# Second attention of a two-block kernel: the row maxima are subtracted by TensorE, and ScalarE copies the context sums

## The chip, the cores and the metric

The kernel runs on one core of one Trainium2 chip. The metric is the device time of one execution in microseconds (us); before the change it is 456.45 us, the median of three runs (454.14 to 458.66). The engines are TensorE (PE, with its weight loads shown apart as PEld), VectorE (DVE), ScalarE (ACT), GpSimd (POOL) and the DMA queue of SyncE (SP). Each engine works through its own list in order, and semaphores tie the lists together.

## The reference

Two transformer-like blocks, each an attention and a mixture of experts, on 2048 tokens of 128 features (8 batches of 256). The change touches the second block's attention alone:

```python
q = (x @ Wq + bq).reshape(b, h, dh, t)      # h = 16 heads, dh = 8
k = (x @ Wk + bk).reshape(b, h, dh, t)
v = (x @ Wv + bv).reshape(b, h, dh, t)
attn = jnp.einsum('bhdt,bhds->bhts', k, v) * temperature
attn = jax.nn.softmax(attn, axis=-1)
out = jnp.einsum('bhdt,bhts->bhds', q, attn)
```

So each of 8 x 16 heads has a score matrix of 256 x 256, a softmax along its rows, and a product with q. The softmax is computed as exp(score - row maximum) over its row sum.

## The kernel before, in words

**Stages.** First attention, first experts, second attention, second experts. All engines' lists are written out by hand; nothing reorders them. The first experts end at about 200 us of the profile, the second attention's exponentials run until about 330 us, and the second experts fill the rest.

**The second attention's loop.** The 128 heads are taken in 32 groups `g` of four heads `j`. A group has two halves of two heads; one half's scores fill two PSUM banks (per head 128 partitions by 2 x 256: `h` is the upper or lower half of the score rows). Three pairs of banks go round (`bank_s1`), so the scores of one half can be written when the exponentials of the half three before it are done. For each half:

- TensorE, `scores` (L1554): four products, two heads by two `h`, contraction over 24 rows, 256 columns each.
- VectorE, `maxima` (L925): one reduction over both banks gives the negated row maxima `nm1` of two heads by two `h`.
- ScalarE (L1208): per head and `h` one exponential of 256 columns with `nm1` as its per-partition bias, and the row sum out of the accumulator, which is a second instruction (ACTIVATION_READ_ACCUMULATOR). So eight such pairs a group.
- VectorE, `denominators` (L933), takes reciprocals of the four heads' sums; GpSimd, `queries` (L526), multiplies them into the weights `qs4`.
- TensorE, `context` (L1566): four products per `h`, each into 32 output partitions of one bank, `BANK_C1`; two calls (`h` = 0 and 1) finish a group.
- VectorE, `outputs` (L940): copies that bank to `O`, from where DMAs take it.

**TensorE's list around the change.** In turn `g` of the loop (L1592): `scores(g+1, 0)`, `context(g-2, 0)`, `scores(g+1, 1)`, `context(g-2, 1)`, and then in some turns one piece of other work (projections, router products, transposes; in the last turn `gate_up(0)` of the second experts comes first). `context(·, 0)` claims `BANK_C1`, that is, it waits until `outputs` of the group before has copied the sums, and then issues four products of ones by ones into the same bank (`dense`, L1301), whose result the context overwrites. VectorE's turn `g` is `outputs(g-3)`, `maxima(g+1, 0)`, `denominators(g-1)`, other work, `maxima(g+1, 1)`. ScalarE's turn is the eight exponentials of group `g`, with other work behind head 1 or head 3 of a few groups (`modulate`, `high_input`, `queries_out`, `weights_out`).

**The start of the loop.** TensorE's list puts `scores(0, 0)`, two steps of the first experts' last products (`down0`), `scores(0, 1)`, three more such steps, `scores(1, 0)` and a projection ahead of turn 0.

Of the kernel before, what the change touches and what calls it, by code (L numbers as in the profile page):

```python
# [17 lines left out]
B, S = 8, 256  # L18
# [15 lines left out]
HPG = 4  # L34
# [12 lines left out]
def two_block_adaln(nc, a, out, scratch):  # L47
# [4 lines left out]
    with ExitStack() as ctx:  # L52
# [31 lines left out]
        ident = sb("ident", [128, 128])  # L84
        ones = sb("ones", [128, 128])
# [17 lines left out]
        def ex1(g, j):  # L103
# [48 lines left out]
        nm1 = sb("nm1", [128, 4, HPG, 2]); Z1 = sb("Z1", [128, 4, HPG, 2])  # L152
# [17 lines left out]
                 "kvs_ready", "s1_ps", "nm1_ready", "e1_ready", "rz_ready", "qs_ready", "c1_ps",  # L170
# [252 lines left out]
        def _(pool):  # L423
# [117 lines left out]

            clear(0)
# [31 lines left out]
        def _(dve):  # L574
# [360 lines left out]
            def outputs(g):  # L935
                b = g // GPB
                dve.wait_ge(s["c1_ps"], g + 1)
                if b >= 2 and g % GPB == 0:
                    dve.wait_ge(ao_out[b - 2], 16 * HPG)
                v.tensor_copy(O[:, b % 2, g % GPB, :], P[:, BANK_C1, 0:S]).then_inc(s["o1_ready"], 1)  # L940

# [3 lines left out]
            for g in range(NG):  # L945
                if g >= 3:
                    outputs(g - 3)
# [35 lines left out]
            outputs(NG - 3)  # L983
# [3 lines left out]
            for n in range(NP * C1):  # L987
                p, i = divmod(n, C1)
                if n in (1, 2):
                    outputs(NG - 3 + n)  # L990
# [33 lines left out]
        def _(act):  # L1024
# [176 lines left out]

            for g in range(NG):
                for j in range(HPG):
                    act.wait_ge(s["nm1_ready"], 2 * g + j // 2 + 1)
                    if g >= 4 and j == 0:
                        act.wait_ge(s["c1_ps"], g - 3)
                    for h in range(2):
                        last = sc.activation(ex1(g, j)[:, h * S:(h + 1) * S],  # L1208
                                             P[:, bank_s1(g, j), h * S:(h + 1) * S],
                                             ACT.Exp, bias=nm1[:, g % 4, j, h:h + 1], accum_out=Z1[:, g % 4, j, h:h + 1])  # L1210
                    last.then_inc(s["e1_ready"], 1)
                    if j == 1 and g == 7:
                        modulate(2, NP - 1)
# [18 lines left out]

            for n in range(NP * C1):
                p, i = divmod(n, C1)
                if i == C1 - 1:
# [30 lines left out]
        def _(pe):  # L1266
# [280 lines left out]
            def scores(g, half):  # L1547
# [3 lines left out]
                for j in (2 * half, 2 * half + 1):  # L1551
                    claim(bank_s1(g, j), "e1_ready", HPG * g + j + 1)
                    for h in range(2):
                        last = mm(P[:, bank_s1(g, j), h * S:(h + 1) * S],  # L1554
                                  KS[32 * j:32 * j + 3 * DH, p % 2, g % GPP, h * D:(h + 1) * D],
                                  VS[32 * j:32 * j + 3 * DH, p % 2, g % GPP, :], start=True, stop=True)
                    last.then_inc(s["s1_ps"], 1)
# [200 lines left out]
```

## Time and profile before

| | |
|---|---|
| median of 3 runs | 456.45 us (454.14 to 458.66) |
| span of the profiled execution, first to last instruction | 453.7 us |
| TensorE busy | 405.5 us (89%) |
| VectorE busy | 360.9 us (80%) |
| ScalarE busy | 329.2 us (73%) |
| GpSimd busy | 253.0 us (56%) |

The page gives the profiled execution's span and no other time of it; the median of the runs is 2.75 us above the span. Busy shares are means over stages with different limits, so the second attention has to be read by itself, from views of 200 to 330 us. In a timeline row the first number is the start in us from the span's start, the second the duration; instructions of one line that follow each other are merged (`x4`). A matmul's recorded end is modelled, and successive matmuls overlap: how fast they follow each other is read from start to start.

### The profile page before, as it was taken

To read this page: it belongs to the slowest core of one execution; us is meant where nothing else is said; L and a number is where in the kernel's file an instruction comes from. 1 tells how busy PE (TensorE), PEld (TensorE's weight loads), DVE (VectorE), ACT (ScalarE), POOL (GpSimd) and SP (SyncE) were. 2 spreads that over 40 slices of the span, in tenths; PEclk is the share of its full clock that TensorE was granted. 3 is DMA by queue.
4 is the path that set the end of the run, shared out by engine and by line. 5 is a ranking of instruction groups with operands and counts; after the bars stand their busy time and mean duration, and the time that the engine had idled before them with its cause. 6 is when DMAs were issued, how large, how long until landed. Compare 5 with 4: busy or idle time off the path is not lost.

```text
span 453.7 us, 7973 instructions
## 1 busy us (share of the span) xinstructions
PE 405.5 (89%) x2328; PEld 272.9 (60%) x2328; DVE 360.9 (80%) x891; ACT 329.2 (73%) x898; POOL 253.0 (56%) x276
## 2 busy tenths in 40 slices
PE   7979878899699798977888888989999999999994
PEld 6667666677487586743333333434467777788782
DVE  5768795876998969869879798898866779778763
ACT  4366558789597686778899899999974575676551
POOL 3302248788786785831353456445357866566653
PEclk9999998999999999989899899999999999999997
DMA  6730031122034043656735245501416433433640
GB/s 180 230 115 4 0 96 46 46 96 70 24 95 111 28 142 115 139 110 96 174 71 105 84 128 91 147 13 25 116 30 183 115 137 100 138 110 99 190 119 23
DMA packets 45819, 44.72 MB, mean 99 GB/s; under 512 B 5700, under 2 KB 33932, under 8 KB 45776
## 3 DMA queue, kind: packets, MB, share of 16 engines
q1 hardware_dynamic: 45776, 44.21, 36.4%
q8 instruction: 19, 0.31, 0.3%
q14 instruction: 24, 0.20, 0.2%
HBM read 37.76 MB, written 6.44 MB: 97 GB/s over the span
## 4 chain that ended last, share of the span: by engine, by line
ACT 25%; PE 15%; DVE 15%; issue 7%; DMA 5%; POOL 3%; SPq 1%; POOLq 0%; DVEq 0%; ACTq 0%
ACT EX L1208 18%; PE P L1279 4%; PE P L1281 4%; PE P L1280 4%; DVE nm L925 3%; DVE P L994 2%; DVE tmp L1002 2%; POOL hidl L482 2%; DVE tmp L887 2%; DMA G<-gate_rows 2%; DMA KS<-kv_parts 2%; ACT hidh L1159 2%; ACT P L1180 1%; PE P L1301 1%; PE P L1554 1%
## 5 line engine op out<-in xcount | busy, mean ns | idle before, releaser
L482 POOL TENSOR_TENSOR hidl<-tmp,hidh 128x512 fp32r<-128x512 f32 x116 | 149.3, 1297 | 68.7 <-ACT hidh L1159 63.4
L1208 ACT ACTIVATE EX<-P,nm 128x256 f32<-128x256 f32 x256 | 117.2, 526 | 6.1 <-DVE nm L925 5.8
L1159 ACT ACTIVATE hidh<-tmp 128x512 fp32r<-128x512 f32 (+1 forms) x116 | 73.0, 630 | 63.4 <-DVE tmp L1002 31.3
L925 DVE TENSOR_REDUCE nm<-P 128x4 f32<-128x1024 f32 x64 | 78.0, 1220 | 16.1 <-PE P L1554 15.6
L1279 PE MATMUL P<-XH,WH 128*128 128x512 f32 x172 | 74.7, 434 | 4.6 <-DVE tmp L887 3.1
L1281 PE MATMUL P<-XL,WH 128*128 128x512 f32 x172 | 68.1, 396 | 0.0
L1280 PE MATMUL P<-XH,WL 128*128 128x512 f32 x172 | 67.8, 394 | 0.0
L1208 ACT ACTIVATION_READ_ACCUMULATOR EX<-P,nm 128x1 f32 x256 | 66.3, 260 | 0.0
L526 POOL TENSOR_TENSOR qs<-qT,rz 128x128 f32<-128x128 f32 x64 | 25.3, 416 | 69.8 <-DVE rz L933 69.8
L887 DVE TENSOR_TENSOR tmp<-P,G 128x512 f32<-128x512 f32 x64 | 43.3, 685 | 19.5 <-issue 9.6
L1279 PE MATMUL P<-hidh,WH 128*128 128x512 f32 (+1 forms) x124 | 50.9, 410 | 3.8 <-POOL hidl L482 3.1
L1281 PE MATMUL P<-hidl,WH 128*128 128x512 f32 (+1 forms) x124 | 49.9, 402 | 0.0
L1280 PE MATMUL P<-hidh,WL 128*128 128x512 f32 (+1 forms) x124 | 49.6, 400 | 0.0
L1301 PE MATMUL P<-ones 128*128 128x512 bf16 x128 | 34.6, 394 | 14.4 <-DVE O L940 13.1
L994 DVE TENSOR_TENSOR P<-wmod,P 128x512 f32<-128x512 f32 (+1 forms) x52 | 36.0, 693 | 13.1 <-ACT wmod L1248 11.3
L1002 DVE TENSOR_TENSOR tmp<-P,G 128x512 f32<-128x512 f32 (+1 forms) x52 | 36.0, 692 | 13.1 <-DMA G<-gate_rows 5.8
L1279 PEld LDWEIGHTS P<-XH,WH 128*128 128x128 f32 x172 | 32.5, 189 | 17.9 <-DVE tmp L887 5.0
L1180 ACT ACTIVATE P<-P,ub 128x512 f32<-128x512 f32 x64 | 41.6, 651 | 0.4 <-PE P L1281 0.4
L1566 PE MATMUL P<-EX,qs 128*32 128x256 f32 x512 | 41.4, 400 | 0.0
L1554 PEld LDWEIGHTS P<-VS,KS 24*128 24x128 f32 x256 | 21.0, 188 | 29.2 <-issue 14.3
L1248 ACT ACTIVATE wmod<-P 128x512 f32<-128x512 f32 x48 | 28.2, 590 | 13.8 <-PE P L1281 13.7
L1554 PE MATMUL P<-VS,KS 24*128 24x256 f32 x256 | 35.0, 336 | 3.1 <-DMA KS<-kv_parts 2.7
(141 smaller groups left out, 696.0 us busy)
## 6 DMA issues: line engine op xcount, KB each, us to landing
G<-gate_rows SPq DMA_DIRECT2D x56, 256.0 KB, 3.2
kv_parts<-kvs SPq DMA_DIRECT2D x16, 256.0 KB, 4.2
VS<-kv_parts SPq DMA_DIRECT2D x48, 64.0 KB
KS<-kv_parts SPq DMA_DIRECT2D x48, 64.0 KB
G<-gate_rows SPq DMA_DIRECT2D x8, 224.0 KB, 2.9
G<-gate_rows SPq DMA_DIRECT2D x8, 192.0 KB, 3.2
G<-gate_rows SPq DMA_DIRECT2D x8, 160.0 KB, 3.4
X<-in_x SPq DMA_DIRECT2D x4, 256.0 KB, 2.9
```

Source lines behind the costliest of these rows:

```text
L482: nc.gpsimd.tensor_tensor(hidl[:, u % 4, :], source, hidh[:, u % 4, :].bitcast(fp32), ALU.subtract).then_inc(s["low_ready"], 1)
L887: v.tensor_tensor(hidf0[:, u % 4, :], P[:, bank_up(u), :], G[:, q % GR, :], ALU.mult).then_inc(s["bc_read"], 1)
L925: v.tensor_reduce(nm1[:, g % 4, 2 * h:2 * h + 2, :], P[:, bank:bank + 2, :].rearrange("p j (h s) -> p (j h) s", h=2), AX.X, ALU.max, negat ...
L994: v.tensor_tensor(P[k, bank_u(n), :], act_out[k, n % 3, :], P[k, bank_u(n), :], ALU.mult).then_inc(s["u_read"], 1)
L1002: v.tensor_tensor(hidf[k, n % 2, :], P[k, bank_u(n), :], G[k, q % GR, :], ALU.mult).then_inc(s["bc_read"], 1)
L1159: sc.activation(hidh[k, u % 4, :], source[k], ACT.Copy).then_inc(s["high_ready"], 1)
L1180: sc.activation(act_out[:, u % 3, :] if i < C0 else P[:, bank_up(u), :], P[:, bank_up(u), :], ACT.Gelu, bias=ub0[:, e, c:c + 1]).then_inc( ...
L1208: last = sc.activation(ex1(g, j)[:, h * S:(h + 1) * S], P[:, bank_s1(g, j), h * S:(h + 1) * S], ACT.Exp, bias=nm1[:, g % 4, j, h:h + 1], a ...
L1279: mm(P[:, bank, :], WH[k, w:w + m], xh, start=start, stop=False)
L1280: mm(P[:, bank, :], WL[k, w:w + m], xh, start=False, stop=False)
L1281: return mm(P[:, bank, :], WH[k, w:w + m], xl, start=False, stop=stop)
L1554: last = mm(P[:, bank_s1(g, j), h * S:(h + 1) * S], KS[32 * j:32 * j + 3 * DH, p % 2, g % GPP, h * D:(h + 1) * D], VS[32 * j:32 * j + 3 * ...
```

## The change

TensorE now subtracts the maxima. A new call `subtract(g, half)` multiplies an identity matrix (`identr`, rounded to fp32r once by GpSimd) with the negated maxima, each repeated over 256 columns, and accumulates the product on top of the scores in PSUM: two products of 512 columns per half. In TensorE's turn `g`, `subtract(g, 1)` stands behind `context(g-2, 0)` and `subtract(g+1, 0)` behind `context(g-2, 1)`; `subtract(0, 0)` stands ahead of the loop behind the last `down0`. ScalarE's exponentials wait for these products (`f1_ps`) and take no bias. The four `dense` products ahead of each context are gone (those of turns 0 and 1 stay). `outputs` moves from VectorE to ScalarE: in group `g` it stands behind head 0. The scores of a half are issued `h` by `h` over its two heads, where before they went head by head.

```diff
-        nm1 = sb("nm1", [128, 4, HPG, 2]); Z1 = sb("Z1", [128, 4, HPG, 2])
+        nm1 = sb("nm1", [128, 4, HPG, 2], fp32r); Z1 = sb("Z1", [128, 4, HPG, 2])
...
+            nc.gpsimd.tensor_copy(identr[:, :], ident[:, :]).then_inc(s["ident_round"], 1)
             clear(0)
...
             for g in range(NG):
-                if g >= 3:
-                    outputs(g - 3)
                 if g + 1 < NG:
                     maxima(g + 1, 0)
...
+            def outputs(g):
+
+                b = g // GPB
+                act.wait_ge(s["c1_ps"], g + 1)
+                if b >= 2 and g % GPB == 0:
+                    act.wait_ge(ao_out[b - 2], 16 * HPG)
+                sc.activation(O[:, b % 2, g % GPB, :], P[:, BANK_C1, 0:S], ACT.Copy).then_inc(s["o1_ready"], 1)
+
             for g in range(NG):
                 for j in range(HPG):
-                    act.wait_ge(s["nm1_ready"], 2 * g + j // 2 + 1)
+                    act.wait_ge(s["f1_ps"], HPG * g + j + 1)
...
-                                             ACT.Exp, bias=nm1[:, g % 4, j, h:h + 1], accum_out=Z1[:, g % 4, j, h:h + 1])
+                                             ACT.Exp, accum_out=Z1[:, g % 4, j, h:h + 1])
                     last.then_inc(s["e1_ready"], 1)
+                    if j == 0 and g >= 3:
+                        outputs(g - 3)
...
+            def subtract(g, half):
+
+                pe.wait_ge(s["nm1_ready"], 2 * g + half + 1)
+                for j in (2 * half, 2 * half + 1):
+                    mm(P[:, bank_s1(g, j), :], identr[:, :],
+                       nm1[:, g % 4, j, :].unsqueeze(2).broadcast_to([128, 2, S]), start=False, stop=True,
+                       skip_group_check=True).then_inc(s["f1_ps"], 1)
 
             def context(g, h):
                 if h == 0:
                     claim(BANK_C1, "o1_ready", g + 1)
-                    for _ in range(HPG if g < NG - 2 else 0):
-                        dense(BANK_C1)
                     pe.wait_ge(s["qs_ready"], g + 1)
...
             for u in range(NP * STEPS0 - 3, NP * STEPS0):
                 down0(u)
+            pe.wait_ge(s["ident_round"], 1)
+            subtract(0, 0)
             scores(1, 0)
...
                     if g >= 2:
                         context(g - 2, half)
+                    if half == 0:
+                        subtract(g, 1)
+                    elif g + 1 < NG:
+                        subtract(g + 1, 0)
```

TensorE's list in the middle of the second attention, before: from the `dense` products of one turn (L1301) through both contexts (L1566) and the scores between and behind them (L1554).

```order
L1301 MATMUL P<-ones 128x512 [waits o1_ready]
L1301 MATMUL P<-ones 128x512 x3
L1566 MATMUL P<-EX,qs 32x256 [waits qs_ready]
L1566 MATMUL P<-EX,qs 32x256 x3
L1554 MATMUL P<-VS,KS 128x256 [waits e1_ready]
L1554 MATMUL P<-VS,KS 128x256
L1554 MATMUL P<-VS,KS 128x256 [waits e1_ready]
L1554 MATMUL P<-VS,KS 128x256
L1566 MATMUL P<-EX,qs 32x256 x4
L1554 MATMUL P<-VS,KS 128x256 [waits e1_ready]
```

The same stretch of TensorE's list now: contexts are L1581, the identity products L1572, the scores L1561.

```order
L1581 MATMUL P<-EX,qs 32x256 [waits qs_ready,o1_ready]
L1581 MATMUL P<-EX,qs 32x256 x3
L1572 MATMUL P<-nm,identr 128x512 [waits nm1_ready]
L1572 MATMUL P<-nm,identr 128x512
L1561 MATMUL P<-VS,KS 128x256 [waits e1_ready]
L1561 MATMUL P<-VS,KS 128x256 x3
L1581 MATMUL P<-EX,qs 32x256 x4
L1572 MATMUL P<-nm,identr 128x512 [waits nm1_ready]
L1572 MATMUL P<-nm,identr 128x512
L1561 MATMUL P<-VS,KS 128x256 [waits e1_ready]
```

The wait for the copied sums (`o1_ready`) has moved from the ones products to the context itself, and each context is followed by two identity products before the next scores.

ScalarE's list in the same place, one group before (head 0 first):

```order
L1208 ACTIVATE EX,Z<-P,nm 128x256 [waits c1_ps,nm1_ready]
L1208 ACTIVATE EX,Z<-P,nm 128x256
L1208 ACTIVATE EX,Z<-P,nm 128x256 [waits nm1_ready]
L1208 ACTIVATE EX,Z<-P,nm 128x256
L1208 ACTIVATE EX,Z<-P,nm 128x256 [waits nm1_ready]
```

and now, with the copy of the sums as L1199:

```order
L1207 ACTIVATE EX,Z<-P 128x256 [waits c1_ps,f1_ps]
L1207 ACTIVATE EX,Z<-P 128x256
L1199 ACTIVATE O<-P 128x256 [waits c1_ps]
L1207 ACTIVATE EX,Z<-P 128x256 [waits f1_ps]
L1207 ACTIVATE EX,Z<-P 128x256
L1207 ACTIVATE EX,Z<-P 128x256 [waits f1_ps]
```

The copy stands behind the two exponentials of head 0, and every head waits for its identity product where it waited for the maxima.

## Rows read from the trace of the kernel before

**Rows 1.** The page's first line.
```profile
span 453.7 us, 7973 instructions
```
**Rows 2.** Windows: length, busy PE PEld DVE ACT POOL, granted clock, DMA share, GB/s.
```profile
200.00:330.00 130.00, 113.04 (x926) 50.04 (x925) 112.18 (x249) 123.84 (x526) 54.81 (x103) 0.97 0.43 94
...
256.00:260.00 4.00, 3.73 (x24) 1.27 (x24) 2.51 (x6) 3.67 (x16) 2.35 (x4) 0.58 0.00 0
```
**Rows 3.** Timeline, ScalarE: first exponential, first of group 3, last of all.
```profile
200.39 0.47 ACT L1208 ACTIVATE EX<-P,nm 128x256 f32<-128x256 f32 x1
...
213.25 0.48 ACT L1208 ACTIVATE EX<-P,nm 128x256 f32<-128x256 f32 x1
...
329.19 0.45 ACT L1208 ACTIVATE EX<-P,nm 128x256 f32<-128x256 f32 x1
```
**Rows 4.** Timeline, all engines: one turn of the loop, from copy to copy.
```profile
272.38 0.41 DVE L940 COPY O<-P 128x256 f32<-128x256 f32 x1
...
272.86 1.04 PE L1301 MATMUL P<-ones 128*128 128x512 bf16 x4 [0.68 <-DVE O L940]
...
272.97 0.47 ACT L1208 ACTIVATE EX<-P,nm 128x256 f32<-128x256 f32 x1
...
273.41 0.47 ACT L1208 ACTIVATE EX<-P,nm 128x256 f32<-128x256 f32 x1
...
273.82 0.64 PE L1566 MATMUL P<-EX,qs 128*32 128x256 f32 x8
...
274.39 0.50 PE L1554 MATMUL P<-VS,KS 24*128 24x256 f32 x4
...
274.82 0.64 PE L1566 MATMUL P<-EX,qs 128*32 128x256 f32 x8
...
274.97 1.23 DVE L925 TENSOR_REDUCE nm<-P 128x4 f32<-128x1024 f32 x1 [0.37 <-PE P L1554]
...
276.11 0.41 DVE L940 COPY O<-P 128x256 f32<-128x256 f32 x1
```
**Rows 5.** View of one line: ScalarE from PSUM with and without a bias (min/median/max ns).
```profile
L1053 ACT ACTIVATE qT<-P,b0q x4: 684/685/687, 16.9 to 49.0; 128x512 f32<-128x512 f32 x4
L1057 ACT ACTIVATE tqT<-P x4: 597/597/602, 18.8 to 50.9; 128x512 f32<-128x512 f32 x4
```
**Rows 6.** Timeline, TensorE: contexts beside 128x128 fp32r products of 512 columns.
```profile
325.30 0.64 PE L1566 MATMUL P<-EX,qs 128*32 128x256 f32 x8
325.87 0.50 PE L1279 MATMUL P<-XH,WH 128*128 128x512 f32 x1
326.20 0.39 PE L1280 MATMUL P<-XH,WL 128*128 128x512 f32 x1
326.43 0.40 PE L1281 MATMUL P<-XL,WH 128*128 128x512 f32 x1
...
330.61 0.40 PE L1281 MATMUL P<-XL,WH 128*128 128x512 f32 x1
330.94 0.42 PE L1566 MATMUL P<-EX,qs 128*32 128x256 f32 x4
```
**Rows 7.** Timeline: a product and the ScalarE instruction that it releases.
```profile
336.15 0.40 PE L1281 MATMUL P<-XL,WH 128*128 128x512 f32 x1
...
336.59 0.60 ACT L1248 ACTIVATE wmod<-P 128x512 f32<-128x512 f32 x1 [0.63 <-PE P L1281]
```
**Rows 8.** Timeline: other work in the loop on ScalarE, then on TensorE.
```profile
281.77 1.03 ACT L1065 ACTIVATE XT<-P,mcol 128x256 f32<-128x256 f32 x2
...
283.37 0.46 ACT L1208 ACTIVATE EX<-P,nm 128x256 f32<-128x256 f32 x1
...
286.58 1.06 PE L1389 MATMUL P<-rw,XT 128*128 128x9 f32 x8
287.57 0.50 PE L1554 MATMUL P<-VS,KS 24*128 24x256 f32 x4
```
**Rows 9.** Timeline, TensorE: the last product of the first experts.
```profile
202.86 0.40 PE L1281 MATMUL P<-hidl,WH 128*128 128x512 f32 x1
```

More of the change, by code:

```diff
@@ L84, in two_block_adaln @@
         ident = sb("ident", [128, 128])
+        identr = sb("identr", [128, 128], fp32r)
         ones = sb("ones", [128, 128])
@@ L169, in two_block_adaln @@
                  "q1_ps", "q1_sb", "kv_ps",
-                 "kvs_ready", "s1_ps", "nm1_ready", "e1_ready", "rz_ready", "qs_ready", "c1_ps",
+                 "kvs_ready", "ident_round", "s1_ps", "nm1_ready", "f1_ps", "e1_ready", "rz_ready", "qs_ready", "c1_ps",
                  "o1_ready", "gated", "x1_ready", "v_step", "pool_const"]
@@ L540, in attention_residual @@
                 nc.gpsimd.tensor_tensor(X[:, ts, :], X[:, ts, :], AO[:, ts, :], ALU.add).then_inc(s["x1_ready"], 1)
+            pool.wait_ge(s["ld_i"], 16 * N_LD["ld_i"])
+            nc.gpsimd.tensor_copy(identr[:, :], ident[:, :]).then_inc(s["ident_round"], 1)
             clear(0)
@@ L933, in denominators @@
                 v.reciprocal(rz1[:, g % 4, :, :], Z1[:, g % 4, :, :]).then_inc(s["rz_ready"], 1)
[L935 to L940, printed above, removed]
             maxima(0, 0)
@@ L982, in _ @@
             denominators(NG - 1)
-            outputs(NG - 3)
             base = NP * STEPS0
@@ L988, in _ @@
                 p, i = divmod(n, C1)
-                if n in (1, 2):
-                    outputs(NG - 3 + n)
                 dve.wait_ge(s["u_ps"], n + 1)
@@ L1231, in high1 @@
                 high_part(base + n, hidf[:, n % 2, :], rows1(n))
+            outputs(NG - 3)
             for n in range(NP * C1):
                 p, i = divmod(n, C1)
+                if n in (1, 2):
+                    outputs(NG - 3 + n)
                 if i == C1 - 1:
@@ L1550, in scores @@
                     pe.wait_ge(kv_in[p], 16 * 6 * HPG)
-                for j in (2 * half, 2 * half + 1):
+                heads = (2 * half, 2 * half + 1)
+                for j in heads:
                     claim(bank_s1(g, j), "e1_ready", HPG * g + j + 1)
-                    for h in range(2):
+                for h in range(2):
+                    for j in heads:
                         last = mm(P[:, bank_s1(g, j), h * S:(h + 1) * S],
                                   KS[32 * j:32 * j + 3 * DH, p % 2, g % GPP, h * D:(h + 1) * D],
-                                  VS[32 * j:32 * j + 3 * DH, p % 2, g % GPP, :], start=True, stop=True)
-                    last.then_inc(s["s1_ps"], 1)
+                                  VS[32 * j:32 * j + 3 * DH, p % 2, g % GPP, :], start=(h == 0), stop=True,
+                                  skip_group_check=True)
+                        if h == 1:
+                            last.then_inc(s["s1_ps"], 1)
+            def subtract(g, half):
[4 more added lines that the diff above has]
+                       skip_group_check=True).then_inc(s["f1_ps"], 1)
             def context(g, h):
```

## The prediction

> **What bounds the kernel now.** I read the page for the span [rows 1], the windows by stretch to find the stage that the change touches, and there the timeline of each engine. Between 200 and 330 us ScalarE is busy 123.8 of 130 us, TensorE 113.0, VectorE 112.2 [rows 2]: ScalarE is nearest to its limit, but two others are close, and a share does not say which wait ends last. The ends of the stage are the first exponential at 200.39 and the last at 329.19 + 0.45 = 329.6 [rows 3]. Group 3 starts at 213.25, so the 29 groups from there take 116.4 us, 4.01 each.
>
> One turn [rows 4] shows what a turn is made of. ScalarE: an exponential and its accumulator read repeat every 273.41 - 272.97 = 0.44, with rounding 0.45 us, so eight need 3.6. But the copy of the sums comes every 276.11 - 272.38 = 3.73 us, and that is a closed chain: copy 0.41, 0.07 to TensorE, ones 0.96 (272.86 to 273.82), context 0.57 (to 274.39), scores to the start of the maxima 0.58 (274.97), maxima 1.23 less 0.09 overlap, next copy. So today two limits lie side by side, ScalarE at 3.6 and this chain at 3.73; the rest up to 4.01 is other work on ScalarE and VectorE and spells of a slower clock.
>
> **The change, part by part.**
>
> *Bias removed (256 exponentials).* ScalarE's 512 columns out of PSUM take 685 ns with a bias operand and 597 without [rows 5]: 0.09 us. An exponential with its read then repeats every 0.45 - 0.09 = 0.36. No row has an exponential without bias; the bounds are a saving of 0 and of 0.09, and I take 0.09 since the two rows of rows 5 differ in nothing else that ScalarE does.
>
> *Copies moved to ScalarE (32).* One row of 256 columns with bias takes 0.47 [rows 4]; less 0.09 it is 0.38. ScalarE's need per group falls to 8 x 0.36 + 0.38 = 3.26. VectorE loses 32 x 0.41 = 13 us of work; I cost that at nothing, since the new chain below holds no VectorE instruction: counted from the first context of a turn, the scores between the contexts start at 1.24, their maxima are done 0.58 + 1.23 later, at 3.05, and their identity products come in the next turn at 3.94 + 0.57 = 4.5. VectorE's other work has these 1.4 us of room.
>
> *Ones removed, identity products added.* Four products of 512 columns go, four come; TensorE's work hardly changes. But the ones stood where TensorE was waiting anyhow, and the identity products stand between the maxima and ScalarE. What counts is the order: `context(g-2, 0)` waits for the copy, the copy stands behind head 0 of group `g`, head 0 waits for `subtract(g, 0)`, and that stands in TensorE's list behind the whole turn before. This is a closed chain again. Its terms:
>
> - context to the identity products behind it: 0.57 (325.30 to 325.87) [rows 6]
> - identity pair to the next scores: 0.34 (325.87 to 326.20) plus 0.33 for changing over (330.61 to 330.94) [rows 6]
> - scores to the second context: 0.43 (274.39 to 274.82) [rows 4]
> - second context to the second identity pair: 0.57
> - first identity product until its end: 0.50 [rows 6]; to ScalarE 0.04 (336.15 + 0.40 to 336.59) [rows 7]
> - head 0: two exponentials with their reads, 2 x 0.36 = 0.72
> - copy 0.38, and to TensorE 0.06 (VectorE's copy took 0.07, 272.79 to 272.86) [rows 4]
>
> Sum: 0.57 + 0.67 + 0.43 + 0.57 + 0.54 + 0.72 + 0.44 = 3.94 us a turn. ScalarE idles in it twice, about 0.5 and 0.25 us, ahead of head 2 and of head 0; TensorE once, about 0.6, ahead of the first context. So the chain at 3.73 gives way to one at 3.94, and ScalarE's saved 0.36 a group becomes idle time.
>
> Here one rule speaks otherwise. After the change-over the first fp32r product of 512 columns ends 0.50 after its start and the second starts 0.34 later, against 0.39 and 0.23 (326.20 to 326.43) within a run [rows 6]: the new weights are not loaded under the change-over. The Trainium skill, page "TensorE: Matmul & The Clock Gate", section "Back-to-back issue gap", gives N/2.4 + 2.5 ns, 216 ns for 512 columns; by it alone the turn would be about 0.24 us shorter. The row is of the same shape in the same place, so I keep the row; the shorter pair is a rival below.
>
> *Other work in the loop.* ScalarE's, behind head 3: twice a modulation with its rounding, 1.60 us (281.77 to 283.37) [rows 8], less the 0.25 idle: 2.7; two single copies of 0.60 to 0.69 [rows 5], less 0.25 each: 0.8. What stands behind head 1 hides in the 0.5. TensorE's: five pieces like the router products, 0.99 (286.58 to 287.57) [rows 8], of which 0.9 is on top and 0.6 hides: 5 x 0.3 = 1.5; `gate_up(0)` in the last turn, six products at 0.23: 1.5 - 0.6 = 0.9. Together 5.9.
>
> *Start and end.* `subtract(0, 0)` stands behind the last `down0`, which starts at 202.86 [rows 9]: + 0.24 + 0.40 + 0.04 gives a first exponential at 203.5, 3.1 late. The first three groups have no context yet and took 4.29 each before; I put them at 3.65 (two maxima of 1.23 and about 1.2 of other VectorE work), which leaves group 3 at 214.4, 1.2 late. At the end the copy of group 29 stands ahead of ScalarE's work for the second experts: 0.4. Behind that TensorE is nearly full, so a later start is a later end.
>
> *Clock.* Between 256 and 260 us the granted clock is 0.58 on the mean [rows 2]: (1 - 0.58) x 4 / 0.5 = 3.4 us at 1.2 instead of 2.4 GHz. TensorE's part of the new chain is 2.7 of 3.94, so a like spell loses about 3.4 x 2.7/3.94 / 2 = 1.2 us. I count one, with bounds of none and three; ones or identity, TensorE streams as many columns a turn as before.
>
> **Sum** from group 3: 29 x 3.94 = 114.3, + 5.9 + 1.2 = 121.4, against 116.4: +5.0; start and end +1.6: +6.6 us. To be set against: some of the other work falls together on both engines in one turn, where it is paid once; I take 0.7 off. That is +5.9 on a span of 453.7; the page shows nothing of what lies around the span, so I add it to the median of the runs, which is 2.75 above the span: 456.45 + 5.9 = **462.3 us**.
>
> **The rivals.**
>
> *A. The chain as summed*, with its other work and clock between 459 and 466.5: chance 0.56. Of it about 0.10 lies below 461.
>
> *B. The identity pair runs like a pair within a run* (the weights are the same in every pair, and they may already be under way during the change-over): the end comes at 0.39, the second product 0.23 later, turn 3.94 - 0.22 = 3.72, and 29 x 0.22 = 6.4 us less: 455.9. For it: equal weights; against it: the row after the change-over [rows 6]. The Trainium skill's gap, above, would give the same. Its own range, with more or less of the other work hidden, is 453 to 459. Chance 0.22.
>
> *C. Faster: ScalarE sets the pace.* If TensorE reached each identity pair before ScalarE runs dry, a group would take 3.26, and with 5 us of other work 29 x 3.26 + 5 = 99.5 instead of 116.4; with +1.6 that is 441 us. It decides as soon as the chain above is under 3.26, so it needs 0.68 us of its terms to be wrong. For it: ScalarE is the busiest engine of the stage now. The Trainium skill, page "ScalarE: Activation LUTs", section "What ACT_TABLE_LOAD costs", puts about 93 ns on each [128,1] pointer operand, and the trace agrees with 88 [rows 5]. Chance of anything faster than 451.9: 0.10.
>
> *D. The bias costs nothing in the pipeline*, that is, pairs still repeat every 0.45. Then head 0 takes 0.90, and a half of four pairs (1.80) ends after the second identity pair is ready, at 2.91 instead of 2.79 of the turn: 2.91 + 0.90 + 0.44 = 4.25, 29 x 0.31 = 9 us more, 471. Against it: rows 5. Chance 0.07.
>
> *E. More slow-clock spells*, three or four: 466 to 470. Chance 0.05.
>
> **The numbers.** The time is that of A. A measurement of this kernel can tell about 1% from no change, 451.9 to 461.0. Faster: C, 0.10. Same: B and the lower part of A, 0.22 + 0.10 = 0.32. Slower: the rest of A, D and E, 0.46 + 0.07 + 0.05 = 0.58. The range leaves out C and D and a little of B's and E's far ends: 453.5 to 467.5.
>
> **What would show it.** Right: copies (ACT, O<-P) every 3.9 us with the context starting 0.05 behind each; ScalarE idle twice a group, released by the identity products; the accumulator read 0.26 behind its exponential's start; first exponential near 203.5; VectorE's waits on scores grown. Wrong: a second identity product 0.22 behind the first (B), ScalarE without gaps between 230 and 320 (C), exponentials still 0.45 apart (D), or VectorE's maxima as what releases the identity products, which I hold to have 1.4 us to spare.

## The result, and the profile after

The changed kernel takes 470.02 us (median of four executions, 466.91 to 471.82) beside 455.94 for the kernel before on the same chip: 1.029 times as long, 95% interval 1.022 to 1.036. The forecast was 462.3 in a range of 453.5 to 467.5: the sign was right, the size was not, and the median lies outside the range. Executions of one version can differ by some per cent, with their mean granted clock, and a ratio is given from the fast ones alone.

The profiled execution has a span of 465.1 us against 453.7 [rows 1], 11.4 more:

```profile
span 465.1 us, 8077 instructions
```

The ends of the stage on ScalarE are the first exponential, the first of group 3 and the last one; they answer to [rows 3].

```profile
204.63 0.38 ACT L1207 ACTIVATE EX<-P 128x256 f32<-128x256 f32 x1 [1.66 <-PE P L1572]
...
215.31 0.38 ACT L1207 ACTIVATE EX<-P 128x256 f32<-128x256 f32 x1
...
340.46 0.38 ACT L1207 ACTIVATE EX<-P 128x256 f32<-128x256 f32 x1
...
340.82 0.38 ACT L1207 ACTIVATE EX<-P 128x256 f32<-128x256 f32 x1
...
341.17 0.39 ACT L1207 ACTIVATE EX<-P 128x256 f32<-128x256 f32 x1
```

The last exponential ends at 341.6, before at 329.6: 11.9 later, so the whole difference arises up to there, and what follows takes as long as before within 0.5 us. Group 3 begins 2.1 later, and the 29 groups from there take 126.3 us instead of 116.4. The last three rows show the pair of exponential and accumulator read at 0.36 and 0.35 apart; before it was 0.44 [rows 4].

One turn, from one copy of the sums (L1199) to the next; it answers to [rows 4]. L1581 are the contexts, L1572 the identity products, L1561 the scores, L928 the maxima.

```profile
262.89 0.38 ACT L1207 ACTIVATE EX<-P 128x256 f32<-128x256 f32 x1
...
263.62 0.38 ACT L1199 ACTIVATE O<-P 128x256 f32<-128x256 f32 x1
...
264.06 0.64 PE L1581 MATMUL P<-EX,qs 128*32 128x256 f32 x8 [0.56 <-ACT O L1199]
...
264.63 0.70 PE L1572 MATMUL P<-nm,identr 128*128 128x512 f32 x2
...
265.15 0.38 ACT L1207 ACTIVATE EX<-P 128x256 f32<-128x256 f32 x1 [0.42 <-PE P L1572]
265.26 0.50 PE L1561 MATMUL P<-VS,KS 24*128 24x256 f32 x4
...
265.69 0.64 PE L1581 MATMUL P<-EX,qs 128*32 128x256 f32 x8
...
266.26 0.70 PE L1572 MATMUL P<-nm,identr 128*128 128x512 f32 x2
...
266.78 0.39 ACT L1207 ACTIVATE EX<-P 128x256 f32<-128x256 f32 x1
...
267.51 0.38 ACT L1199 ACTIVATE O<-P 128x256 f32<-128x256 f32 x1
```

This is the chain as the forecast has it, term by term: context to identity pair 0.57, pair to scores 0.63 (forecast 0.67), scores to context 0.43, context to the second pair 0.57, to ScalarE 0.52 (0.54), head 0 0.73 (0.72), copy and on to TensorE 0.44. Sum 3.89, and the copies are 3.89 apart. The waits inside the stage answer to it. In these rows stand the engine and line that waited, what ended the wait, us in total, how often, and the longest.

```profile
DVE nm L928 <- PE P L1561: 31.1, 38, 2.9
...
ACT EX L1207 <- PE P L1572: 24.8, 35, 2.6
...
PE P L1581 <- ACT O L1199: 12.8, 17, 2.0
...
PEld P L1572 <- DVE nm L928: 2.3, 5, 0.6
```

ScalarE waits for identity products, TensorE for the copy, and the maxima hardly hold up anybody. What the forecast doesn't have shows in the windows (columns as in rows 2; the granted clock is the number behind POOL's):

```profile
205.00:345.00 140.00, 125.84 (x946) 61.57 (x944) 102.25 (x216) 115.11 (x558) 55.07 (x103) 0.93 0.39 86
247.00:275.00 28.00, 24.68 (x206) 11.56 (x204) 23.85 (x45) 24.34 (x123) 14.14 (x25) 1.00 0.46 112
280.00:290.00 10.00, 8.05 (x62) 4.73 (x54) 5.28 (x10) 8.53 (x39) 3.08 (x7) 0.84 0.44 108
290.00:300.00 10.00, 10.00 (x58) 4.36 (x57) 5.17 (x15) 4.73 (x25) 4.17 (x7) 0.65 0.31 79
300.00:310.00 10.00, 8.99 (x56) 3.81 (x56) 7.70 (x26) 7.65 (x38) 3.81 (x8) 0.69 0.04 13
310.00:320.00 10.00, 8.05 (x55) 3.89 (x48) 6.12 (x15) 6.76 (x30) 2.62 (x7) 0.80 0.02 3
```

From 205 to 280 us TensorE has 2.4 GHz. Between 280 and 320 the mean is 0.745, that is (1 - 0.745) x 40 / 0.5 = 20 us at 1.2 GHz; in the trace these are two spells of 10.2 us, from 286.8 and from 303.9. Between 290 and 300 TensorE has no idle time, and ScalarE is busy less than half of it. The first spell comes 2 us behind this wait of TensorE, which the timeline shows:

```profile
282.14 1.04 ACT L1056 ACTIVATE XT<-P,mcol 128x256 f32<-128x256 f32 x2
...
283.21 0.63 ACT L1066 ACTIVATE XH<-XT 128x512 fp32r<-128x512 f32 x1
...
284.45 0.38 ACT L1199 ACTIVATE O<-P 128x256 f32<-128x256 f32 x1
...
284.89 0.64 PE L1581 MATMUL P<-EX,qs 128*32 128x256 f32 x8 [1.95 <-ACT O L1199]
```

ScalarE's modulation and rounding behind group 19 hold back head 0, head 0 the copy, and the copy TensorE, for 1.95 us. The second spell comes 1.9 us behind a wait of 0.95 us. But the same pieces behind group 25 make TensorE wait 1.95 us once more, until 318.8, and no spell follows that wait.

### The profile page after: what moved, and what is told of

Same layout as the page of the kernel before. It is cut to its first block, busy times and chain, and to the rows that moved or that the text cites. A ratio compares the mean times of both kernels' runs of the same rounds, so it can differ in the third digit from the quotient of the medians.

```text
span 465.1 us, 8077 instructions
## 1 busy us (share of the span) xinstructions
PE 422.9 (91%) x2336; PEld 288.8 (62%) x2336; DVE 350.9 (75%) x859; ACT 319.4 (69%) x930; POOL 253.3 (54%) x277
## 4 chain that ended last, share of the span: by engine, by line
PE 31%; ACT 14%; issue 12%; DVE 11%; POOL 10%; DMA 3%; SPq 1%; POOLq 0%; DVEq 0%; ACTq 0%
POOL hidl L483 9%; PE P L1581 8%; PE P L1572 7%; ACT EX L1207 5%; PE P L1561 4%; PE P L1283 3%; DVE tmp L890 3%; PE P L1285 3%; PE P L1284 3%; ACT hidh L1150 3%; ACT P L1171 2%; DMA KS<-kv_parts 2%; ACT O L1199 1%; ACT XT L1056 1%; PE P L1425 1%
## 5 line engine op out<-in xcount | busy, mean ns | idle before, releaser
L1207 ACT ACTIVATE EX<-P 128x256 f32<-128x256 f32 x256 | 95.3, 388 | 26.1 <-PE P L1572 24.8
L928 DVE TENSOR_REDUCE nm<-P 128x4 fp32r<-128x1024 f32 x64 | 77.9, 1222 | 32.0 <-PE P L1561 31.3
L1581 PE MATMUL P<-EX,qs 128*32 128x256 f32 x512 | 43.2, 414 | 13.2 <-ACT O L1199 12.8
L1207 ACT ACTIVATION_READ_ACCUMULATOR EX<-P 128x1 f32 x256 | 54.4, 212 | 0.0
L1572 PE MATMUL P<-nm,identr 128*128 128x512 f32 x128 | 48.0, 459 | 0.3 <-DVE nm L928 0.2
L1572 PEld LDWEIGHTS P<-nm,identr 128*128 128x128 f32 x128 | 20.4, 199 | 27.8 <-issue 25.2
L1285 PEld LDWEIGHTS P<-XL,WH 128*128 128x128 f32 x172 | 32.7, 190 | 7.6
```

The source lines that it names most:

```text
L928: v.tensor_reduce(nm1[:, g % 4, 2 * h:2 * h + 2, :], P[:, bank:bank + 2, :].rearrange("p j (h s) -> p (j h) s", h=2), AX.X, ALU.max, negat ...
L1207: last = sc.activation(ex1(g, j)[:, h * S:(h + 1) * S], P[:, bank_s1(g, j), h * S:(h + 1) * S], ACT.Exp, accum_out=Z1[:, g % 4, j, h:h + 1])
L1285: return mm(P[:, bank, :], WH[k, w:w + m], xl, start=False, stop=stop)
L1572: mm(P[:, bank_s1(g, j), :], identr[:, :], nm1[:, g % 4, j, :].unsqueeze(2).broadcast_to([128, 2, S]), start=False, stop=True, skip_group_ ...
L1581: last = mm(P[32 * j:32 * j + 32, BANK_C1, 0:S], qs4[:, g % 2, j, h, :, :].rearrange("p r d -> p (r d)"), ex1(g, j)[:, h * S:(h + 1) * S], ...
```

## The experiments

Theory 1: the turn is a closed chain from the copy through TensorE and head 0 back to the copy, and what the kernel takes beyond the forecast are the spells at 1.2 GHz. Rivals: the identity products cost more by themselves, or the missing ones products let the clock fall. Twelve kernels were run, each in four executions beside the kernel before.

**The copy back on VectorE.** `outputs` stands in VectorE's list again; everything else is as changed.

The first lines are in VectorE's list, the last in ScalarE's; `...` marks what is left out.

```diff
+                if g >= 3:
+                    outputs(g - 3)
...
-                    if j == 0 and g >= 3:
-                        outputs(g - 3)
...
```

> The change with one part undone: VectorE copies the context sums again, as before, and everything else is as in the changed kernel. Theory 1 (the turn is a closed chain that runs through head 0's exponentials and ScalarE's copy; what came on top of the forecast are two spells of 10.2 us at 1.2 GHz, which follow long waits of TensorE for that copy): the chain is cut. TensorE's own turn is left, 0.57 + 0.67 + 0.43 twice over = 3.35 us, or VectorE's chain, scores to maxima 0.58 + 1.14 + copy 0.41 + 0.06 + context 0.57 + identity 0.67 = 3.43; a turn of 3.4 to 3.6 instead of 3.89, TensorE without waits over 1 us, no spell of 10 us: 448 to 458 us. Rival (the identity products themselves are what costs, TensorE's list is too long whoever copies): turn stays at 3.8 to 3.9, 462 to 468 us. Rival (the slow clock comes of the ones products that are gone): turn 3.4 to 3.6, but spells of 10 us stay, 458 to 464 us.

Measured: 457.94 us, ratio to before 1.005 (0.999 to 1.011). That is 12 us less than the changed kernel: ScalarE's copy was worth the larger part of the loss. At full clock most turns take 3.4 to 3.9 us. With this one part undone and the identity products kept, the kernel is not slower than before, so the products by themselves are not the loss. The median lies at the edge between the two ranges; the profiled execution (474.84, the longest of the four) holds spells of 23.9 and 30.7 us, in which a turn takes 5.77.

**The modulations spread.** ScalarE's two modulations and roundings stand in three pieces behind head 1 of three groups, not behind head 3 of one.

```diff
+                    if j == 1 and g in (19, 25):
+                        modulate(3, g // 25, (0,))
+                    if j == 1 and g in (20, 26):
+                        modulate(3, g // 26, (1,))
+                    if j == 1 and g in (21, 27):
+                        high_input(1, g // 27)
...
-                        if g in (19, 25):
-                            modulate(3, g // 25)
-                            high_input(1, g // 25)
```

> The changed kernel with ScalarE's two other pieces spread: the two halves of each modulation and its rounding stand behind head 1 of three groups in a row, one piece of 0.45 to 0.52 us each, where both stood behind head 3 of one group (1.6 us together). Theory 1 (the two spells at 1.2 GHz follow TensorE's wait of about 2 us for the copy behind these pieces): the pieces fall into ScalarE's idle 0.5 us ahead of head 2, the wait of 2 us is gone, and with it at least the first spell: turns of 3.9 throughout, 2.7 us less for the pieces and 4 to 8 us less for the spells, 459 to 463 us. Rival (the spells come of the short wait in every turn, about 0.6 us, that the ones products used to fill): the spells stay, only the 2.7 us go, 466 to 468 us.

Measured: 455.94 us, ratio to before 0.999 (0.993 to 1.006): 14 us less than the changed kernel, more than expected, with the chain untouched. The pieces hide: groups 19, 20 and 21 take 3.89, 3.89 and 4.06 us. The other work that no longer stands on the path is 2 x 1.4 = 2.8 us (group 19 took 5.30 in the changed kernel), and most of the rest of the 14 goes with the clock: three of the four executions have a mean of 0.98 and take 453.4 to 457.0, the changed kernel's four have 0.95 to 0.96. The fourth (471.61, the profiled one) holds a spell of 47.8 us. It shows the price, before it and in it:

```profile
220.00:280.00 60.00, 53.68 (x450) 25.63 (x450) 48.28 (x85) 53.52 (x266) 30.62 (x57) 1.00 0.46 93
300.00:340.00 40.00, 39.84 (x194) 18.54 (x196) 20.33 (x63) 23.95 (x115) 12.74 (x23) 0.50 0.15 37
```

Two copies, in the spell:

```profile
298.02 0.38 ACT L1200 ACTIVATE O<-P 128x256 f32<-128x256 f32 x1
...
303.91 0.38 ACT L1200 ACTIVATE O<-P 128x256 f32<-128x256 f32 x1
```

A turn without other work takes 5.89 us there instead of 3.89, so in such turns a spell costs (5.89 - 3.89)/5.89 = 0.34 of its length, and TensorE has next to no idle time.

**The copy ahead of head 0.**

```diff
                 for j in range(HPG):
+                    if j == 0 and g >= 3:
+                        outputs(g - 3)
                     act.wait_ge(s["f1_ps"], HPG * g + j + 1)
...
-                    if j == 0 and g >= 3:
-                        outputs(g - 3)
```

> The changed kernel with ScalarE's copy one place earlier: ahead of head 0 of the group instead of behind it. No other difference. Theory 1 (the chain runs through head 0): 0.72 us of head 0 leave the chain, ScalarE is idle at that place anyhow, and the copy is done before TensorE reaches the context; TensorE's own turn of 3.35 us sets the pace, 3.4 to 3.5, TensorE has no wait left for the copy, no long spell at 1.2 GHz: 29 x 0.45 = 13 us less and up to 8 us less for the clock, 448 to 456 us. Rival (the identity products are what costs, with no closed chain through ScalarE): no difference, 467 to 471 us.

Measured: 459.37 us, four executions from 448.4 (mean clock 0.986) to 466.29 (0.938), too far apart for a ratio. Two copies of the profiled execution at full clock:

```profile
260.25 0.40 ACT L1199 ACTIVATE O<-P 128x256 f32<-128x256 f32 x1
...
263.51 0.40 ACT L1199 ACTIVATE O<-P 128x256 f32<-128x256 f32 x1
```

A turn of 3.26 instead of 3.89: head 0 did stand in the chain. That is ScalarE's own need as the forecast worked it out (8 x 0.36 + 0.38). The median still lies above the theory's range. In the profiled execution what spoils it is a wait of TensorE of 4.2 us later in the stage, in which a spell of 34 us begins; in that spell a plain turn takes 5.77 us, so here a spell costs (5.77 - 3.26)/5.77 = 0.43 of its length.

**The kernel before without its ones products.** Only the four ones products of a turn are left out, which is no part of the result.

```diff
                     claim(BANK_C1, "o1_ready", g + 1)
-                    for _ in range(HPG if g < NG - 2 else 0):
-                        dense(BANK_C1)
```

> The kernel before with one part of the change: the four ones products ahead of each context are gone, all else is as before. They are no part of the result. Theory 1 (in the kernel before, the ones stand in a closed chain of 3.73 us through VectorE's copy, and the slow clock of the changed kernel is not their absence): 0.97 us leave that chain, ScalarE's 3.6 sets the pace, 29 x 0.1 = 3 us less, the clock as before or one more spell: 451 to 457 us. Rival (the ones hold TensorE's clock up): spells of 10 us at 1.2 GHz appear between 200 and 330 us; there TensorE's shorter list has room, so 456 to 465 us.

Measured: 462.42 us, ratio 1.0155 (1.010 to 1.021), and one spell of 105.8 us, besides one of 6.8 ahead of it and one of 10.2 behind it:

```profile
220.00:320.00 100.00, 95.63 (x608) 41.85 (x610) 82.22 (x177) 93.02 (x393) 44.26 (x81) 0.50 0.37 90
```

All four executions have a mean clock of 0.85 to 0.87, where the kernel before has 0.97 to 0.99. So in the order of work before, the ones products do keep TensorE at 2.4 GHz for most of the stage. But the price differs: with over 100 us at 1.2 GHz the kernel loses 6.5 us net of what the shorter list may save, 0.06 of the spell. ScalarE covers it: a group without other work takes 3.60 us in the spell, and 3.59 in the kernel before.

**Ones products in TensorE's waiting time.** Two of the four are back, ahead of the next group's scores and in the banks that those overwrite.

```diff
                     claim(bank_s1(g, j), "e1_ready", HPG * g + j + 1)
+                for _ in range(2 if half == 0 and 3 <= g else 0):
+                    dense(bank_s1(g, 0))
                 for h in range(2):
```

> The changed kernel with two of the four ones products of a turn put back, not behind the copy but ahead of the scores of the next group, into the banks that those scores overwrite. TensorE waits there some 0.6 us a turn for the copy, and two ones products fill about 0.48 of it, so the chain should stay at 3.9 to 4.0 us a turn. Theory (the excess over the forecast is two spells at 1.2 GHz, started by TensorE standing idle): with the idle time filled the clock holds in most of the stage and the 8 us come back: 460 to 465 us. Rival (the spells have nothing to do with the ones, or only the two long waits of 2.2 and 1.2 us start them, which two ones products don't fill): 468 to 474 us, with two spells of 10 us or more in the trace as before.

Measured: 470.71 us, ratio 1.029 (1.020 to 1.038), as without them. In a plain turn they fill the wait at no cost, as TensorE's timeline shows (L1305 the ones, L1583 the contexts):

```profile
263.02 0.70 PE L1574 MATMUL P<-nm,identr 128*128 128x512 f32 x2
263.62 0.59 PE L1305 MATMUL P<-ones 128*128 128x512 bf16 x2
264.14 0.50 PE L1563 MATMUL P<-VS,KS 24*128 24x256 f32 x4
264.70 0.64 PE L1583 MATMUL P<-EX,qs 128*32 128x256 f32 x8
```

The turn stays at 3.89, TensorE is busy 27.6 of 28 us between 247 and 275, and still a spell of 13.7 us comes from 286.7, behind a wait of 1.46 us at the same modulation as before. Filling the short waits of every turn does not hold the clock through a long one. The theory's number (460 to 465) was wrong; the rival's range of times was right, though there is one spell of over 10 us and not two. The time alone does not tell what the ones did to the clock: in groups with other work they cost time (group 8 takes 4.56 us instead of 3.99), and the three executions in the ratio have mean clocks of 0.968 to 0.979, where the changed kernel's have 0.948 to 0.959.

**Copy first and the spread together.** Both diffs above.

> The changed kernel with the copy of the sums ahead of head 0 and the modulations and roundings of groups 19 and 25 spread over three groups behind head 1. Theory: the first takes head 0 out of the closed chain (turn 3.3 us at full clock, seen with the copy first alone), the second takes away the two long waits of TensorE that started the spells; together 440 to 450 us with at most one short spell. Rival (without the ones products the clock falls sooner or later whatever the waits): a spell of 20 us or more stays, 455 to 465 us.

Measured: 455.97 us median, with executions at 443.88 and 444.78 (mean clock 0.99) and at 467.15 and 470.55 (0.93); ratio of the two at 0.99 to the kernel before 0.974 (0.965 to 0.982). Two executions have the theory's number; the median and the profiled execution's spell are the rival's. GpSimd's timeline of that execution has the cause of the long wait in it:

```profile
288.20 0.72 POOL L537 TENSOR_TENSOR SC<-SC,mrow 128x256 f32<-128x256 f32 x1 [7.04 <-DMA SC<-attention_rows]
...
290.90 0.76 POOL L527 TENSOR_TENSOR qs<-qT,rz 128x128 f32<-128x128 f32 x2
```

The faster turns arrive at the gated residual of batch 3 before its rows have come back from memory; GpSimd waits 7.0 us, the weights of the next contexts are queued behind it, TensorE stands for 5.5, and in that wait a spell of 54.6 us begins. What the two short executions did there has no trace.

**Copy on VectorE and the spread.**

> The changed kernel with the copy on VectorE as it was before and the same spread of the modulations. Theory: turn of 3.45 to 3.9 us at full clock, long waits gone, 448 to 455 us. Rival (copy back on VectorE delays the maxima, which then release the identity products): no gain over the copy on VectorE alone, 456 to 460 us.

Measured: 450.98 us, executions from 449.03 to 453.44, ratio 0.988 (0.981 to 0.995). All four have a mean clock of 0.98 to 0.99, and the profiled one has no spell in the stage:

```profile
205.00:325.00 120.00, 111.49 (x911) 54.32 (x909) 107.94 (x241) 102.64 (x516) 54.46 (x101) 1.00 0.44 99
```

No version above had four such executions: the identity products with the copy where it was, and the modulations spread, are 1.2% faster than the kernel before. TensorE's longest wait in the stage is 1.01 us here.

**The kernel before with the spread.**

> The kernel before with the same spread of the modulations, as a control: what the spread is worth without the identity products. Theory (in the kernel before the clock is held by the ones products, and the modulations cost only their own time on ScalarE, 2 x 1.6 us less what hides): 452 to 456 us. Rival (the spread is worth its 14 us in any version): 440 to 445 us.

Measured: 456.18 us, ratio 0.996 (0.987 to 1.005). The spread is worth nothing there and 14 us in the changed kernel: most of what it takes away is not the work but what the work does to TensorE in the closed chain. The profiled execution (456.16) shows something besides: behind a wait of TensorE of 2.17 us until 213.6 comes a spell of 10.2 us, as long as those of the changed kernel, with all the ones products in place and no identity product.

```profile
213.00:223.00 10.00, 9.42 (x48) 3.70 (x48) 8.20 (x19) 8.05 (x36) 1.53 (x4) 0.52 0.80 202
```

**Copy first and the spread, with the long wait shortened.** GpSimd's residual of batch 3, VectorE's normalisation of it and ScalarE's one query projection are moved, the first by one group, the others within theirs or by a few instructions.

```diff
-                    if i in (10, 12):
-                        attention_residual(2 * p + i // 2 - 5)
+                    if (p, g) in ((0, 10), (0, 12), (1, 18), (1, 21)):
+                        attention_residual(2 * p + (g in (12, 21)))
...
```

> The version with the copy first and the spread modulations, with three steps of the normalisation moved: GpSimd's gated residual of batch 3 stands one group later (it waited 7.0 us for its rows there, with the weights of the contexts queued behind it, and TensorE stood 5.5 us), VectorE's statistics and scaling of that batch behind the second maxima of their group, GpSimd's root behind the weights; and ScalarE's one query projection of group 22 from head 3 to behind head 1. Theory (long waits of TensorE start the spells, nothing else): the wait of 5.5 us shrinks to 2 us or less, no spell of over 10 us in most runs, 440 to 448 us. Rival (without the ones products the clock falls sooner or later): as without the moves, runs between 444 and 470 us with a median near 455.

Measured: 448.63 us, 0.6 above the theory's range, ratio 0.984 (0.978 to 0.991): executions at 445.77, 447.62 and 449.63, and one (the profiled) at 469.02, which has a wait of 2.2 us left (VectorE's maxima behind its wait for the residual) and a spell of 47.8 us that begins in it. The best version of these twelve by its median, but not a safe one.

**One pause, in two kernels.** ScalarE makes seven small copies, one after another, behind the last head of group 12, into a tile that the next group overwrites: first in the version with the copy on VectorE and the spread, then in the kernel before.

```diff
+                    if j == HPG - 1 and g == 12:
+                        act.wait_ge(s["c1_ps"], g - 2)
+                        for i in range(7):
+                            sc.activation(ex1(g + 1, 0)[:, 0:D], ones[:, :], ACT.Copy).then_inc(s["pause"], 1)
+                            act.wait_ge(s["pause"], i + 1)
```

> The version with the copy on VectorE and the spread modulations, whose stage ran without any spell, with one pause on ScalarE added behind the last head of group 12: seven small copies one after another, some 2.5 us, and nothing else. Theory (one long wait of TensorE starts a spell, and the chain through TensorE then keeps the loss): a spell of 6.8 us or more begins within 3 us of TensorE's wait, and the time grows by the pause and 4 to 15 us more: 456 to 468 us. Rival (waits don't start spells): the pause alone, 452 to 455 us.

> The kernel before with the same pause of some 2.5 us on ScalarE behind group 12. ScalarE is nearest to its limit there, so the pause itself costs its full length. Theory (the ones products bring the clock back soon, and ScalarE's need of 3.6 us a turn hides what TensorE loses): a spell of 3.4 us or none, 458 to 460 us beside a before of 456. Rival (a wait costs as much with the ones products): 462 to 470 us.

The pause and the wait of TensorE behind it, first with the identity products:

```profile
252.40 2.37 ACT L1219 ACTIVATE EX<-ones 128x128 f32<-128x128 f32 x7
...
254.20 0.64 PE L1589 MATMUL P<-EX,qs 128*32 128x256 f32 x8 [1.00 <-DVE O L943]
```

and in the kernel before:

```profile
252.34 2.37 ACT L1215 ACTIVATE EX<-ones 128x128 f32<-128x128 f32 x7
...
255.53 1.04 PE L1306 MATMUL P<-ones 128*128 128x512 bf16 x4 [1.30 <-DVE O L940]
```

With the identity products: 451.07 in the profiled execution, which has no spell (so here the wait started none, and the time is even below the rival's), but 464.01, 469.40 and 486.22 in the others, with mean clocks of 0.96, 0.94 and 0.89; without the pause all four were below 453.5. No ratio can be given. In the kernel before: 453.93 us, ratio 0.999 (0.995 to 1.004), four executions within 2.4 us; below what either theory gave, since groups 13 to 18 behind the pause took 3.60 each, where in the kernel before they took 3.73 to 5.01, and gave its length back. The same pause is harmless in the one kernel, and in the other it came with three long executions of four. But the pause is no test of a long wait of TensorE: in neither trace does it give a longer one than there was without it (1.00 and 1.04 us beside 1.01 with the identity products, 1.30 beside 1.30 in the kernel before). That a wait only makes a spell likelier fits the four executions, but they are few, and the three long ones have no trace.

**The removal alone undone.** The four ones products of a turn are back where they stood.

```diff
                     claim(BANK_C1, "o1_ready", g + 1)
+                    for _ in range(HPG if g < NG - 2 else 0):
+                        dense(BANK_C1)
```

> The changed kernel with the four ones products of a turn put back where they stood before, behind the wait for the copied sums; nothing else undone. Theory (the turn is a closed chain from the copy through TensorE, head 0 and back to the copy): the ones now stand in that chain, so every turn is 0.97 us longer, 4.86 us at full clock, 29 x 0.97 = 28 us, less up to 7 us if they hold the clock: 488 to 498 us. Rival (the removal of the ones is what made the changed kernel slow, and they cost nothing while TensorE waits): 456 to 464 us. The spells in the trace tell besides whether four ones products a turn hold the clock in this order of the work: none over 3.4 us if they do, two of 10 us or more if the long waits of TensorE decide alone.

Measured: 492.15 us, ratio 1.082 (1.074 to 1.089), the theory's number. Two copies:

```profile
268.56 0.38 ACT L1199 ACTIVATE O<-P 128x256 f32<-128x256 f32 x1
...
273.42 0.38 ACT L1199 ACTIVATE O<-P 128x256 f32<-128x256 f32 x1
```

4.86 us a turn: the 0.97 of the ones goes wholly into the chain. From group 3 to the last exponential the profiled execution takes 152.5 us, 26.2 more than the changed kernel's. And the windows behind the modulation show a fall of the clock all the same, a spell of 13.7 us from 298.6:

```profile
280.00:300.00 20.00, 16.81 (x130) 7.46 (x123) 11.52 (x19) 14.87 (x71) 9.67 (x19) 0.96 0.51 95
300.00:320.00 20.00, 19.69 (x106) 8.97 (x104) 7.91 (x17) 9.73 (x49) 5.21 (x8) 0.69 0.18 46
```

So the changed kernel would gain nothing by the ones products in this place: with them it is slower, and the clock falls behind the long wait anyhow. They may still shorten the spells: the mean clocks of the four are 0.964 to 0.982, the changed kernel's 0.948 to 0.959, and the spells in this trace's stage are 13.7 and 3.4 us.

## Why the prediction missed

**The chain was right.** 3.94 was forecast and 3.89 measured, with no term off by more than 0.04. Copy first (3.26) and the ones put back (4.86) show it from both sides: taking head 0 out shortens the turn, and what is put between the copy and the context lengthens it by its own length. The change-over ahead of an fp32r product was rightly kept from the row and not from the gap within a run: pair to scores 0.63, where rival B had 0.22 less in the turn.

**The bias was right.** Pairs are 0.36 apart as forecast; rival D had them at 0.45. The Trainium skill, page "ScalarE: Activation LUTs", section "What ACT_TABLE_LOAD costs", has about 93 ns for such an operand; the rows show 0.44 - 0.36 = 0.08, within their rounding.

**The other work was right**: 5.9 forecast, less 0.7 for what falls together, 5.2. Group by group at full clock it comes to 5.1, an estimate: groups 3 to 19 and 26 to 31 are the changed kernel's own, group 25 is put at the 5.30 of group 19, and 20 to 24 are taken from the spread version and the version with two ones products.

**The start was 1.1 us short.** The last step of the first experts began at 203.99 and not at 202.86 [rows 9]; the first exponential follows 0.64 behind its start, as forecast (0.68). This is the execution's and not the change's: in the profiles of other versions with the same start the first exponential comes between 201.9 and 203.5. Group 3 was 0.9 later than forecast (215.3 for 214.4).

**The clock failed.** The step reads: "I count one, with bounds of none and three; ones or identity, TensorE streams as many columns a turn as before." One spell of 3.4 us was counted, 1.2 us of loss; there were two of 10.2. With 29 x 3.89 + 5.1 = 117.9 us from group 3 on the stage would have ended at 215.3 + 117.9 = 333.2; it ended at 341.6, so they cost about 8.4 us. The loss lies in groups 20 to 25, between the first exponentials of group 20 and of group 26:

```profile
283.74 0.36 ACT L1207 ACTIVATE EX<-P 128x256 f32<-128x256 f32 x1
...
317.68 0.36 ACT L1207 ACTIVATE EX<-P 128x256 f32<-128x256 f32 x1
```

They take 33.9 us. In the spread version groups 20 to 22 run at full clock (first exponentials of groups 20 and 23):

```profile
280.17 0.39 ACT L1208 ACTIVATE EX<-P 128x256 f32<-128x256 f32 x1
...
292.62 0.41 ACT L1208 ACTIVATE EX<-P 128x256 f32<-128x256 f32 x1
```

That is 12.45 us; with 3.9 each for groups 23 and 24, as in the version with two ones products, and 5.3 for group 25 it makes 25.5, which is 8.4 less.

The price that the forecast put on a spell, 2.7/3.94/2 = 0.34 of its length, is what a plain turn of the spread version shows. This is in part luck: the forecast has TensorE busy for 0.69 of a spell, and the rows have it busy throughout (39.84 of 40 us). Over the two spells, which also hold groups with other work, the price is 8.4/20.5 = 0.41; at 0.34 they would have cost 7.0. So the mis-sized factor is above all the length of the spells, 20.5 us in place of 3.4, and with it the bound "three" (10.2). Even the trace before has two spells from group 3 on, at 215.7 and 256.6 us, of which one was counted.

Rival E had 466 to 470 for three or four spells, at a chance of 0.05. That the median comes to 470.0 is luck for its number: at the forecast's 1.2 us each, three or four spells give 465 to 466, and what came was two spells, each three times as long. With 8.4 instead of 1.2 the sum of the prediction gives 469.5; a chain 29 x 0.05 = 1.4 shorter and a group 3 that comes 0.9 later make it 469.0. These terms are from the profiled execution, which is the shortest of the four (466.91); the others have no trace.

The reason behind the step failed too. It equated the columns that TensorE streams with the clock that it is given. In the traces spells of very different lengths come with the same columns a turn, and a wait does not fix the length either. In the kernel before a wait of TensorE of 2.2 us ahead of 214 us was followed by 3.4 us at 1.2 GHz, and in the kernel before with the spread the same wait by 10.2. In the changed kernel one wait of 1.95 us was followed by 10.2 us and another of 1.95 by none, and in other versions with identity products waits of 0.7 to 5.5 us by 13.7 to 54.6.

What does differ is the cover. Before, ScalarE's 3.60 us a turn stood beside TensorE and took up most of a spell (6.5 us net for 105.8 without the ones products; the execution of the kernel before with a spell of 10.2 us took 456.16, no more than its median). Now the products of both halves lie in the closed chain. The Trainium skill, page "TensorE: Matmul & The Clock Gate", section "Terms", puts the penalty at the throttled time times the missing share, which is half at 1.2 GHz. The runs have less: 0.34 in a plain turn of the changed order, 0.41 over its two spells, 0.43 with the copy first, and 0.06 net where ScalarE covers it.

**What stays open.** Why a spell lasts 3.4 us in one execution and 50 in another is not settled; in some long ones TensorE has next to no idle time (47.6 of 47.8 us busy in the spread version's), so idle time does not keep those going. Nor is it settled that a long wait starts them: every spell of 10 us or more in the profiles of the versions with identity products begins in a wait of TensorE of 0.7 us or more or within 2 us behind one, and taking away the long waits at the modulations gave 14 us back. But the second wait of 1.95 us in the changed kernel started none, nor did one of 1.46 us until 318.6 in the version with two ones products, waits of 1.0 us stand in the trace of the version without a spell, and the one pause that was put in made no longer wait to test it with.

## What to carry to other kernels

When a change moves work into a closed chain through TensorE, look for the places where another engine's occasional work holds that chain back, and spread that work out: here it was worth 14 us in the changed kernel and nothing in the kernel before. Price a spell of the slower clock by whether another engine covers it, and put the bound of its length at tens of us, not at the spells of one trace of the kernel before. And before a copy is moved to the engine with room to spare, see what stands ahead of it in that engine's list: the same copy one head earlier takes 0.63 us off every turn.

## What the runs showed of the hardware

- TensorE stayed at 1.2 GHz for 105.8 us while it was busy 95.6 of 100 us (the kernel before without ones products), and for 47.8 us in a version that had run 60 us at 2.4 GHz with idle time in every turn.
- On ScalarE a copy of 256 columns out of PSUM that shows a duration of 0.38 us delays the next exponential by 0.27 only: in the changed kernel it starts at 263.62, the exponential behind it at 263.89.
- An identity product of 512 columns behind a context ends 0.48 us after its start, and the second of the pair starts 0.32 behind the first, though both have the same weights.
